# The front of the first layer as entries of the first attention's table, loads in order of use, and another order at the boundary to the FFN

## What is computed

```python
x = x + ln(attn0(ln(x)));  x = x + ln(ffn0(ln(x)))
x = x + ln(attn1(ln(x)));  x = x + ln(ffn1(ln(x)))

# attn0: 16 heads of 16, latents for queries (85) and keys/values (128)
c_q = layernorm(x @ W_d_q.T + b_d_q, q_norm_g, q_norm_b)
q = c_q @ W_u_q.T + b_u_q                # per head: 8 plain, 8 rotary
c_kv = x @ W_d_kv.T + b_d_kv             # 128 latent + 8 rotary, one for all heads
kv_n = layernorm(c_kv[..., :128], kv_norm_g, kv_norm_b)
kv = kv_n @ W_u_kv.T + b_u_kv            # per head: 8 of the key, 16 values
y = softmax(causal(q_full @ k_full.T / 4)) @ v
return y @ W_o.T + b_o
# attn1: q, k, v = x @ w_qkv.T + b_qkv, the same causal attention, @ w_out.T + b_out
# ffn: (silu(x@w_gate*s_gate) * (x@w_up*s_up)) @ w_dn * s_down, int8 weights
```

## Time and profile before

| | us | share of the span |
|---|---|---|
| median of 3 runs | 1214.76 (1214.48 to 1216.93) | |
| the profiled execution | 1218.57 | |
| its span | 1216.8 | |
| PE busy | 1135.3 | 93% |
| DVE busy | 1025.0 | 84% |
| ACT busy | 779.6 | 64% |
| POOL busy | 341.9 | 28% |

### The profile page before, as it was taken

One profiled execution on the slowest core, in us unless ns is written; L12 is line 12 of the kernel. 1 busy time (PEld: TensorE's weight loads), 2 busy tenths in 40 slices (PEclk: granted clock), 3 DMA queues, 4 the chain that ended last, 5 costly groups with the idle time before them and its releaser, 6 DMA issues.

```text
span 1216.8 us, 36838 instructions
## 1 busy us (share of the span) xinstructions
PE 1135.3 (93%) x14888; PEld 573.3 (47%) x14888; DVE 1025.0 (84%) x2714; ACT 779.6 (64%) x1565; POOL 341.9 (28%) x579
## 2 busy tenths in 40 slices
PE   4768999999999999899998989999999999999996
PEld 3532334445444444655654334444444444465664
DVE  6859999999999784777877999999989888648776
ACT  2452668887888989335452456878888888944332
POOL 5232210121211124343442321113121112434443
PEclk9986999999999999999998999999999999999998
DMA  5263100211200000010220340041120000000001
GB/s 181 78 208 96 60 11 12 68 29 28 55 3 3 3 3 4 1 36 14 66 78 29 107 118 29 7 110 35 29 55 3 3 3 4 4 1 1 18 18 35
DMA packets 31611, 50.03 MB, mean 41 GB/s; under 512 B 7246, under 2 KB 24144, under 8 KB 31432
## 3 DMA queue, kind: packets, MB, share of 16 engines
q1 hardware_dynamic: 25376, 41.95, 12.3%
q0 software_dynamic: 5488, 5.34, 1.6%
q10 hardware_dynamic: 576, 0.39, 0.1%
HBM read 32.56 MB, written 14.68 MB: 39 GB/s over the span
## 4 chain that ended last, share of the span: by engine, by line
PE 68%; DVE 20%; issue 3%; ACT 3%; DMA 2%; POOL 2%; ACTq 0%; POOLq 0%; DVEq 0%
PE ps L1095 66%; DVE m_tile L962 6%; DVE ps L964 3%; PE ps L1269 1%; DVE stats L805 1%; ACT region_p L733 1%; DVE region_p L842 1%; DVE region_p L1016 1%; DVE k_stack L1048 1%; DMA q_stack<-m_rows 1%; PE ps L1090 1%; DVE k_stack L1045 1%; DMA q_parts<-parts 1%; DVE rem L859 1%; DVE region_p L818 1%
## 5 line engine op out<-in xcount | busy, mean ns | idle before, releaser
L733 ACT ACTIVATE region_p<-ps 128x512 f32<-128x512 f32 (+3 forms) x1280 | 591.9, 538 | 158.1 <-PE ps L1095 153.5
L962 DVE TENSOR_REDUCE m_tile<-ps 128x1 f32<-128x512 f32 x768 | 497.6, 684 | 27.4 <-PE ps L1095 24.8
L1095 PE MATMUL ps<-k_stack,q_stack 96*32 96x512 bf16 (+3 forms) x5120 | 400.5, 355 | 14.2 <-DVE m_tile L962 3.8
L1095 PE MATMUL ps<-q_stack,k_stack 99*32 99x512 bf16 (+3 forms) x5120 | 400.1, 349 | 9.2 <-ACT region_p L733 3.8
L1095 PE MATMUL ps<-region_p,v_all 128*17 128x512 f32 (+3 forms) x2560 | 290.2, 529 | 0.5 <-POOL region_p L610 0.5
L964 DVE CUSTOM_DVE_ANT_0 ps<-ps,causal 128x128 f32<-128x128 f32 (+3 forms) x512 | 247.5, 499 | 23.2 <-PE ps L1095 21.5
L1095 PEld LDWEIGHTS ps<-k_stack,q_stack 96*32 96x32 bf16 x5120 | 138.1, 96 | 198.2 <-DVE m_tile L962 61.1
L1095 PEld LDWEIGHTS ps<-q_stack,k_stack 99*32 99x32 bf16 x5120 | 138.1, 96 | 194.1 <-ACT region_p L733 108.5
L610 POOL TENSOR_SCALAR_AFFINE_SELECT region_p<-region_p 128x512 f32<-128x512 f32 x128 | 81.2, 635 | 250.5 <-ACT region_p L733 242.4
L1095 PE MATMUL ps<-region_a,w_ffn 128*128 128x512 f16 x512 | 123.7, 387 | 6.1 <-DVE region_a L850 6.1
L769 ACT ACTIVATE k_stack<-ps,cols 128x512 f32<-128x512 f32 x64 | 44.1, 688 | 109.0 <-PE ps L1095 104.1
(11 more groups left out here) (125 smaller groups left out, 887.1 us busy)
## 6 DMA issues: line engine op xcount, KB each, us to landing
k_parts<-parts SPq DMA_DIRECT2D x16, 384.0 KB, 2.5
q_parts<-parts SPq DMA_DIRECT2D x16, 384.0 KB, 3.2
q_stack<-q_parts SPq DMA_DIRECT2D x32, 192.0 KB
k_stack<-k_parts SPq DMA_DIRECT2D x32, 192.0 KB
q_stack<-q_parts SPq DMA_DIRECT2D x32, 128.0 KB
k_stack<-k_parts SPq DMA_DIRECT2D x32, 128.0 KB
X<-in_x SPq DMA_DIRECT2D x4, 512.0 KB, 6.9
q_stack<-q_parts SPq DMA_DIRECT2D x32, 64.0 KB
```

Source lines behind the costliest of these rows:

```text
L733: nc.scalar.activation(probs[:, o.j % SLOTS, o.h, o.off:CH], psT[:, o.k % TBANKS, o.off:CH], ACT.Exp, scale=SCALE).then_inc(s.exp_done, 1)
L962: nc.vector.tensor_reduce(maximum, scores, AX.X, ALU.max).then_inc(s.ring_free, 1)
L1095: return pe.matmul(o, a, b, start=first, stop=last)
```

## The change

1. **Table.** `TURNS` is new: the front of layer 0 is in it, as letters g (statistics of a chunk of x), n (its normalization), x (two transposes and their moves), d (down product and statistics of two tiles), q (root), z (normalization of a chunk's latents), i, j (transposes of the two latents), u, r, m, v, w. x, d, i, j, u and v take a bank of the ring of four each. The `*_BEFORE` lists are gone; units and values stand among the scores. `TURNS_1` is as it was.
2. **Front.** Down and value bias come by PE, as `pick` times bf16 parts (`bd_parts`, `bv_parts`), which POOL makes by `split_row`; the down products stay in PSUM, DVE takes their statistics there, and ACT normalizes them (two tiles: DVE). ACT evacuates layer 0's values and also scales `ckv_t`. The queries' weights are rotated by POOL. Normalized x is in `w_ffn`, the normalized latents in the second half of `k_stack`.
3. **Loads.** `w_down` and `w_kr` are loaded by SP after the first quarter of x; causal after ACT's first root; a dummy root comes first; rotary for 85 partitions; rows in two loads; ones for the second half and the FFN's raw weights behind the last latent. The keys and queries of the second half have semaphores of their own, and `load_second_group` sets their order.
4. **Conversion.** `convert_ffn` stands in steps 5 to 7 in layer 0 too.
5. **MT** is four transposes of 32 columns each, instead of one of 128.
6. **Boundary** (both layers). `o_move(6)` comes ahead of `sqrt_branch(1)`; ACT normalizes the four tiles of chunk 1 (`shift` = -mean * rstd, by DVE's `output_shift`); DVE does `output_shift` ahead of `stats_residual` of chunk 0, and `o_stats(3)` ahead of `low_parts`.

```diff
 TURNS = (
-    "SSSSSSSSSSSSSSSSSSSSMSSSSSSSSSSSSSSSTTSSSTTTSSSSTTTSSTSSVSSSTSSSTSTSSTTMSTTSVSSSSSSVSSSVSSTSSTSS"
+    "gnxxggddquznrjmnxixxugrxurmddmqzddqznujrSiSSmiSSuurmSrxSSSmSxSSSSjSSddquzruMvwmrSSSSSuSrmvSwSmSS"
+    "iSSSSSSSSTSTTSSSSuSTrSTvwmTSSSTTSSuSrSvwSSSjSMSSSSTmSSTTVSTTSuSvTrSSSwSVSSSSmTTuTSvrwSTSTSTSVSTS"
...
+IN_BANKS = "SMYxuvdij"
...
             for g in range(4):
                 sp.dma_start(X[:, 4 * g:4 * g + 4, :], xin[:, 4 * g:4 * g + 4, :]).then_inc(x_in[g], 16)
+                if g == 0:
+                    sp.dma_start(w_down, D["w_down"]).then_inc(w_first, 16)
+                    sp.dma_start(w_kr, D["w_kr"]).then_inc(w_first, 16)
...
+            pool.wait_ge(rows_first, 16)
+            split_row(bd_parts, row("b_down"), proj[0].b_down)
+            pool.wait_ge(x_in[1], 16)
+            load_weights(0)
+            pool.dma_start(rows[:, DQ + DKV:], D["rows"][:, DQ + DKV:].broadcast_to([P, NROWS - DQ - DKV])).then_inc(rows_in, 16)
+            load_ones(0)
+            nc.gpsimd.memset(v_all[:, :, :, DH:VW], 1.0).then_inc(s.v_ones, 1)
+            rotate_queries()
+            pool.wait_ge(rows_in, 16)
+            split_row(bv_parts, row("b_v", 0), proj[0].b_v)
+            split_row(bo_parts[:, 0, :, :], row("b_o", 0), oproj[0].bias)
+            split_row(bo_parts[:, 1, :, :], row("b_o", 1), oproj[1].bias)
...
+            if o.kind == "DOWN":
+                return proj[0].z, 2 * TPC * (o.k // 2 + 1)
...
-                        if L == 1 and 5 <= o.n < 8:
-                            convert_ffn(1, (o.n - 5,))
+                        if 5 <= o.n < 8:
+                            convert_ffn(L, (o.n - 5,))
...
                 o_move(5)
+                o_move(6)
                 sqrt_branch(k1, 1)
-                o_move(6)
+                act.wait_ge(turn[k1].rstd_done, 3)
+                for i in range(TPC, 2 * TPC):
+                    nc.scalar.activation(A[:, i, :], o_tile(i), ACT.Identity, scale=rstd[:, i, 0:1], bias=shift[:, i, 0:1]
+                                         ).then_inc(turn[k1].normed, 1)
...
                 o_stats(1)
+                output_shift(1)
                 stats_residual(k1, 0)
-                normalize_output(1)
                 normalize_residual(k1, 0)
                 o_stats(2)
                 normalize_output(2)
+                o_stats(3)
                 low_parts(k1, 0)
-                o_stats(3)
                 normalize_output(3)
...
-                        pe.transpose(ps[:, RING0 + o.ring % RING, 0:P // 2].bitcast(BF16),
-                                     m_parts[:, o.n % 2, :], ident_bf[:]).then_inc(s.ring_filled, 1)
+                        column_transposes(ps[:, RING0 + o.ring % RING, 0:P // 2].bitcast(BF16),
+                                          m_parts[:, o.n % 2, :], ident_bf[:]).then_inc(s.ring_filled, 1)
```

More of the change, by code:

```diff
@@ L179, in build_program @@
     IN_RING = [{o.ring: o for o in order if o.ring is not None} for order in ORDERS]
-    SIDE_RING = {(o.kind, o.k): o.ring for o in ORDERS[1] if o.kind in ("X", "U", "V")}
+    SIDE_RING = [{(o.kind, o.k): o.ring for o in order if o.ring is not None and o.seq is None} for order in ORDERS]
+    FRONT_READ = max(n for n, o in enumerate(ORDERS[0]) if o.kind in ("QT", "KVT"))
     CHUNK_2_READ = max(n for n, o in enumerate(ORDERS[1]) if (o.kind, o.k) in (("U", 11), ("V", 5)))
@@ L1101, in column_tiles, with column_transposes @@
                 return ins
+            def column_transposes(o, a, identity):
+                for j in range(P // 32):
+                    ins = pe.transpose(o[32 * j:32 * j + 32], a[:, 32 * j:32 * j + 32], identity)
+                return ins
             def unit_products(L, u):
@@ L1200, in _, with latent_transposes @@
+                def latent_transposes(kind, c, half, done):
+                    pe.wait_ge(proj[0].z, 2 * TPC * (c + 1))
+                    for t in range(TPC):
+                        ins = pe.transpose(z_bank(kind, c)[0:half.stop - half.start, t * P:(t + 1) * P],
+                                           c_down[:, TPC * c + t, half], ident[:])
+                    ins.then_inc(done, 1)
+                if L == 1:
                     pe.wait_ge(turn[2].moved_a, 6)
```

481 lines of the change are left out of this document (241 added, 240 removed).

## The result

The changed kernel takes 1220.22 us (median of 18 runs, 1215.37 to 1226.60), the one before 1215.99 beside it (18 runs, 1213.98 to 1220.32): ratio 1.0039, 95% interval 1.0029 to 1.0050. It is 4.2 us slower, where 15.5 us faster was forecast and 1187 to 1209 given as the range. The two profiled executions differ by less (1219.71 and 1218.57; spans 1217.7 and 1216.8), so the traces account for 1 of the 4 us.

What follows compares the result with a forecast made beforehand. Idle waits bound the front, DVE's maxima the scores to 350 us, PE the rest of layer 0's attention. -33.2 + 10 + 5.7 + 3.5 - 1.5 = -15.5 from 1214.76 gave 1199.3 us; range 1187 to 1209.

Steps and rivals of the forecast that it cites:

- First score product: Front of layer 0: the first score product starts at 42.5 us, 44 us earlier; 40 to 47 at the ends.
- To the first MT: Layer 0, from first score product to first MT transpose: MT at 62.5 us against 95.7, a gain of 33.2.
- the 58 to 66: Sign to look for: layer 0's first MT transpose starts between 58 and 66 us.
- MT 0 to MT 4: Layer 0's attention between these transposes: moved work costs +10 us, ends 6.7 and 14.3.
- layer 1's 14.3: Before the change, layer 1 takes 14.3 us more than layer 0 between these transposes; scaled by DVE's work to +10.
- rival A: Layer 0's attention: PE bounds throughout and the front's work, about 28 us, is appended; 1206.5 us, chance 0.17.
- Rival D: Layer 0's scores: front entries hold one of four ring banks and the maxima wait; slower, 1233 us, chance 0.08.
- MT 4 to the end of the attention: Layer 0: converting FFN weights on ACT costs +5.7 us up to MT 8, nothing from there to the end.
- The boundary: Attention to FFN, both layers: DVE waits for ACT's root, first gate product later; +1.6 and +1.9, together +3.5 us.
- MT in strips: MT transposes as four column strips: they cost PE less where it bounds; -1.5 us, at most -2.7.
- the boundary's own: Upper end of the cost forecast at the boundary to the FFN, both layers: +5.4 us; the lower end was -3.8.

Runs made afterwards that it cites:

- e4: Changed kernel with layer 0's values taken out of PSUM by DVE instead of ACT: 1228.4 us, ratio 1.0100 to the kernel before.
- f4: Changed kernel with each MT as one transpose of 128 columns, as before the change: 1223.9 us, ratio 1.0070 to the kernel before.
- f1: Changed kernel with POOL's two splits of b_o moved to where it waits for the maxima of step 10: 1216.7 us, ratio 1.0013 to the kernel before.

## Why the prediction was wrong

Point by point, by its steps:

- **First score product**: 42.5 forecast, 48.07. POOL's chain held to 0.4 us. The step that failed is "and the last takes about 2": 7.66 us. The earlier trace rows had landings of 2.8 and 5.6, and I had named the late end, 47. From 44 to 46.5 us the DMA share is 0.15 and from 46.5 to 48 it is 0.05, so 2.4 of 16 engines and then fewer are at work: the end is not the volume but what a few engines still hold. Which of the loads that is, and why, was not tried.
- **To the first MT**: 20 us from the first score product forecast, 21.3, with PE waiting 2.6 us for ACT's normalization of the latents, as forecast. MT 0 at 69.4, outside the 58 to 66 that I had named: -26.3 where the sum has -33.2.
- **MT 0 to MT 4**: +10 forecast, +16.5. This is the step that decided. I took layer 1's 14.3 and cut it in proportion to DVE's side work. The earlier trace rows showed PE at 97% as well, and rival A had counted what the entries cost PE: 28 us in all. The measured growth of PE's busy time from the first score product to the end is 420.3 - 392.2 = 28.1. Rival A's account, that PE pays in full for what is moved behind the start, comes nearest, at a chance of 0.17; with its start 5.6 later its 1206.5 would have been 1212.1, where the traces give 1214.76 + 0.9 = 1215.7. That PE is the only bound, as A has it, e4 contradicts. Rival D, the ring of banks, is not what made the stretch longer: PE waits for DVE's maxima 3.3 us from MT 0 to MT 4 before the change and 1.2 after it. The size is uncertain by some us, since kernels with the same work took 13.8 to 18.9 more than the kernel before; the +10 lies outside of all.
- **MT 4 to the end of the attention**: +5.7 for the conversion up to MT 8 and nothing behind. It was +1.9 and +3.9, 5.8 in all; 4.3 of it are waits for ACT behind the three pieces. Right in sum, but two thirds of it lie behind MT 8, where I had taken nothing, so the sum is in part luck.
- **The boundary**: +3.5 forecast. The first gate product came 2.4 and 2.6 us later, and undoing it gave 4.7. The traces have +0.6 and +2.9 in the stretches that hold the two, 3.5 in sum, where +1.6 and +1.9 were forecast; in other executions with the new order layer 0's stretch is up to 2.5 longer than before, so the exact 3.5 is luck. The wait of DVE, its cause and its place were as forecast.
- **MT in strips**: -1.5 forecast, -3.7 by f4, with an interval that reaches down to 1.6. I let half hide in the DVE-bound part and behind others; whether less hides is not settled.
- **Sum** of the traces: -26.3 + 16.5 + 5.8 = -4.0 at MT 15 of layer 0; +0.6 to layer 1's first MT, +1.4 in its attention, +2.9 behind it: +0.9. The +1.4 is no more than executions differ by: layer 1's attention, whose table no kernel changes, takes 396.6 to 401.2 us in those with strips.

So the forecast failed on two terms of 6 to 7 us each: the landing of the last stack load, put at 2 us and measured at 7.66, with 1.3 more to MT 0, and the price of side work from MT 0 to MT 4, read from DVE's work as +10 and measured at +16.5 with PE's work. The rest is two of 1.5 us (the strips, whose gain is already in the stretches' lengths, and layer 1's attention). For both large ones the text named an end nearer to what came (a start at 47, layer 1's whole 14.3), and the nearer row was passed over each time. Those ends together with the boundary's own give 1199.3 + 4.5 + 4.3 + 1.9 = 1210, beyond the 1209 of the range: terms that are all bounded on the same side were treated as if their errors would cancel. The balance of PE ties them together: 26.0 us of work ahead of the first score product and 420.3 behind it, so a microsecond by which the start is late or PE waits goes into the end almost undiminished, as f1's 5.7 at the first score product and 5.3 at MT 15 show.

## What to carry to other kernels

Work that is moved from an idle front into a loop with two full engines is not hidden: price it on each of them by the rows of that loop, and take the larger. In this kernel the gain of such a move was only the idle time of PE, the fullest engine, that went away; count it ahead of the new start and behind it. When something is moved off the path, look up what stands behind it in its new place: the two splits, 7.5 us of POOL, cost about 5 us ahead of the first low part, 6 to 7 in front of the maxima's loads, and nothing that the trace shows in a stretch where POOL waits. And take differences of a few us from medians of many runs: single traces of the same instructions differed by 5 us in one stretch here.
